# Keys and values of the first four pairs of a key-masked cross-attention made inside the recurrence sublayer before it

## The reference, cut to what matters

```python
x = x + rwkv(_layernorm(x), ...)                  # recurrence sublayer
x = x + xattn(_layernorm(x), ctx, ctx, mask, ...) # key-masked attention, 16 heads of 16

# xattn, per batch
q = (layernorm(x) @ Wq + bq) * 0.25
k = ctx @ Wk + bk          # depends on ctx and weights alone
v = ctx @ Wv + bv          # the same
p = softmax(q k^T + mask)  # per head
x = x + (p @ v) @ Wo + bo
```

## Time and profile before

| | us |
|---|---|
| median of 3 runs | 2873.56 (2870.24 to 2874.7) |
| the profiled execution's own time | 2876.9 |
| its span in the profile | 2875.1 |
| recurrence block, to the barrier behind it | some 245 |
| key-masked attention block, first steps' maxima to the last | 258.46 to 415.28 |
| busy over the span: TensorE, VectorE, ScalarE, GpSimd | 89%, 59%, 44%, 30% |

### The profile page before, as it was taken

The page is one execution under the profiler, slowest core; times in us unless marked ns, Lnnn a source line. Parts: engine busy times, 40 slices in busy tenths (PEclk is TensorE's granted clock), DMA queues, the critical chain, the costliest instruction groups (busy, mean ns, idle before and its releaser), DMA issues. The chain is left out here.

```text
span 2875.1 us, 49084 instructions
## 1 busy us (share of the span) xinstructions
PE 2545.3 (89%) x16401; PEld 1829.6 (64%) x16401; DVE 1705.5 (59%) x4509; ACT 1260.0 (44%) x3451; POOL 855.4 (30%) x687
## 2 busy tenths in 40 slices
PE   4998998989799889599998998978969899869997
PEld 2665665766544356477776776757956567449996
DVE  7875986588766644344445557873336578434443
ACT  2333654256455323444443445743432388324342
POOL 4533440045431044122221225641110044132222
PEclk8999999999899899799999999978989999989998
DMA  9001000000300333200001002042130210531110
GB/s 319 14 1 51 14 2 19 1 16 1 83 11 1 60 94 113 96 1 1 1 1 47 18 1 75 1 161 76 38 93 1 58 44 5 191 118 49 54 51 26
DMA packets 155268, 144.06 MB, mean 50 GB/s; under 512 B 62024, under 2 KB 139982, under 8 KB 154640
## 3 DMA queue, kind: packets, MB, share of 16 engines
q1 hardware_dynamic: 142880, 112.17, 13.6%
q0 software_dynamic: 10560, 27.19, 2.8%
q10 hardware_dynamic: 1584, 1.57, 0.2%
HBM read 99.70 MB, written 43.02 MB: 50 GB/s over the span
## 5 line engine op out<-in xcount | busy, mean ns | idle before, releaser
L979 POOL TENSOR_TENSOR room<-room 128x1024 f32<-128x1024 f32 x144 | 273.8, 1902 | 410.7 <-DVE room L912 410.6
L1454 PE MATMUL l3f_out<-room,Y 128*128 x624 | 141.0, 379 | 0.0
L906 DVE TENSOR_REDUCE room<-room 128x8 f32<-128x1024 f32 (+1 forms) x144 | 140.3, 975 | 0.8 <-ACT room L1057 0.8
L979 POOL TENSOR_TENSOR room<-room,Y 128x1024 f32<-128x1024 f32 x32 | 60.7, 1896 | 232.6 <-DVE Y L912 232.6
L3626 DVE SCALAR_TENSOR_TENSOR room<-l1x_v,room 128x512 f32<-128x512 f32 x128 | 86.9, 685 | 67.9 <-ACT room L3772 67.7
L1454 PEld LDWEIGHTS l3f_out<-room,Y 128*128 128x128 f32 x624 | 115.6, 190 | 14.2
L3772 ACT ACTIVATE room<-l1x_u 128x512 f32<-128x512 f32 x128 | 76.1, 598 | 77.2 <-PE l1x_v L3441 76.8
L1055 ACT ACTIVATE room<-l2a_scores,Y 128x128 f32<-128x128 f32 x256 | 71.0, 379 | 75.3 <-DVE Y L898 75.2
L1055 ACT ACTIVATE room<-l1a_scores,room 128x128 f32<-128x128 f32 x256 | 71.4, 386 | 58.3 <-DVE room L898 58.3
L1055 ACT ACTIVATE room<-l0x_scores,room 128x128 f32<-128x128 f32 x256 | 70.5, 384 | 59.2 <-DVE room L898 59.2
L623 PE MATMUL l2a_proj<-room 128*128 128x256 f32 x384 | 93.9, 387 | 0.0
(11 more groups left out here) (879 smaller groups left out, 6924.2 us busy)
## 6 DMA issues: line engine op xcount, KB each, us to landing
sorted_rows<-head SPq DMA_DIRECT2D x1, 16640.0 KB, 57.6
room<-in_L_ffn_w SPq DMA_DIRECT2D x16, 1024.0 KB, 12.6
room<-in_L_ffn_W SPq DMA_DIRECT2D x16, 1024.0 KB, 12.6
room<-in_ctx SPq DMA_DIRECT2D x32, 256.0 KB, 3.4
Y<-sorted_rows SPq DMA_DIRECT2D x62, 130.0 KB, 2.1
room<-sorted_rows SPq DMA_DIRECT2D x39, 130.0 KB, 2.1
room<-results SPq DMA_DIRECT2D x8, 512.0 KB, 7.1
room<-in_L_ffn_routed_w SPq DMA_DIRECT2D x4, 512.0 KB
```

The source lines that it names most:

```text
L906: dve.tensor_reduce(rsum[:, u % 2, 0:SUMMED], p[:, u % (TURN + 1), 0:SUMMED, :], AX.X, ALU.add)
L979: pool.tensor_tensor(p[:, u % (TURN + 1), :, :], p[:, u % (TURN + 1), :, :], rinv[:, u % (TURN + 1), :].unsqueeze(2).to_broadcast([P, HEAD ...
L1454: mm = pe.matmul(obank[n % 2][:, 0:D], hT[:, n % 2, f, :], chip.room[:, bass.ds(at + (SLOT // 2 + f * D), D)], start=(f == 0), stop=(f == ...
```

## The change

Three places change. In the recurrence block, the context rows of batches 0 to 7 (four pairs) and the attention's weights are loaded ahead of the zeroing transfer. TensorE transposes the rows (16 transposes), makes keys and values of the four pairs (eight products of eight instructions), and ScalarE copies them to new tiles `early_k` and `early_v` (8 copies of 128x512, and 4 of the transposed rows). Products 0 to 5 stand between `kvr(0, 1)` and `out(0, 0)`; products 6 and 7 stand on TensorE behind `out(0, 3)` and ahead of the transposes of group 1, and their copies stand on ScalarE behind the roots of the statistics and ahead of the squares of y. The rows and their transposes lie in `k2`, which is not in use yet.

In the attention block TensorE and ScalarE leave out c, k and v of pairs 0 to 3. VectorE's spreading of the keys (eight tensor_scalar) and its adding of the bias to the values (two tensor_tensor) stay, at the same places of the order, but read `early_k` and `early_v` in SBUF, and signal `spread`. SP loads no context rows for those pairs.

```diff
+    made = EARLY if t_ == "l0x" else 0                       # EARLY = 4
+    early_made = lambda x: x[0] < made and x[1][0] in "ckv"
...
         def wait_emptied(eng, x):
+            if early_made(x):
+                eng.wait_ge(spread, counted[x])
+                return
...
                 def load(g):
-                    if ctxsrc:
-                        if g >= 2:
+                    if ctxsrc and g >= made:
+                        if g >= made + 2:
...
                 def project(x):                              # TensorE
+                    if early_made(x):
+                        return
...
                 def empty(x):                                # VectorE
                     g, (kind, i) = x
-                    bank = wait_filled(dve, x)
-                    m = number[x]
+                    if early_made(x):
+                        bank, signal = (w.early_k if kind == "k" else w.early_v)[:, g, :], spread
+                    else:
+                        bank, m = wait_filled(dve, x), number[x]
+                        signal = emptied[m % 2]
...
                 def empty(x):                                # ScalarE
+                    if early_made(x):
+                        return
...
@@ rwkv_block
+        early_bank = [bank[i] for i in (5, 6, 7, 5, 6, 7, 7, 7)]
+        early_front = {3: 0, 4: 1, 5: 2, 6: 5, 7: 6}
...
             def _(sp):
                 w.load(sp, slice(3, None))
                 w.load_later(sp, chip.later_loaded)
+                prefetch.load(sp)
+                for g in range(EARLY):
+                    sp.dma_start(early_rows[:, g, :, :], chip.ins["ctx_1024"][g * PAIR:(g + 1) * PAIR].rearrange("b s d -> s b d")).then_inc(early_loaded, 16)
                 sp.dma_start(chip.sorted_rows.rearrange("(t p) d -> p t d", p=P), ...).then_inc(chip.rows_zeroed, 16)
-                if prefetch:
-                    prefetch.load(sp)
...
+                def turn_early(g):                           # TensorE
+                    pe.wait_ge(early_loaded, 16 * EARLY)
+                    if g < 2:
+                        pe.wait_ge(emptied[g], 1)
+                    else:
+                        pe.wait_ge(early_rowsT, g - 1)
...
+                def early_product(n):
+                    g, to = n // 2, early_bank[n]
+                    if n == 0:
+                        nw.wait(pe)
+                    if n in early_front:
+                        pe.wait_ge(early_kept, early_front[n] + 1)
+                    pe.wait_ge(early_rowsT, g + 1)
...
                 def out(a, j):
                     if n == 0:
                         pe.wait_ge(chip.later_loaded, 16 * len(w.later))
+                        pe.wait_ge(early_kept, 5)
...
                     if a < NG:
                         kvr(a, 1)
+                    if a == 0:
+                        turn_early(0)
+                        turn_early(1)
+                        for g in range(3):
+                            early_product(2 * g)
+                            early_product(2 * g + 1)
+                            if g + 2 < EARLY:
+                                turn_early(g + 2)
...
                         for j in range(GR):
                             out(a, j)
                     if a == 0:
+                        early_product(6)
+                        early_product(7)
+                        pe.wait_ge(early_rowsT, EARLY)
                         pe.wait_ge(hn1_ready, 2)
                         transposes(hn1, t1_fill(1))
...
                         exps(a, 1)                           # ScalarE
+                    if a == 0:
+                        keep_rowsT(0)
+                        keep_rowsT(1)
+                        for g in range(3):
+                            keep(2 * g)
+                            keep(2 * g + 1)
+                            if g + 2 < EARLY:
+                                keep_rowsT(g + 2)
...
                     act.preload_act_table(ACT.Sqrt)
                     if t == 0:
                         stats(slice(GR, NB), s[1])
+                        keep(6)
+                        keep(7)
```

More of the change, by code:

```diff
@@ L390 @@
 UNIT = 4
+EARLY = 4
 def attention_block(chip, plan, w, prefetch, have_stats, leave_twice):
@@ L451, in attention_block @@
             for x in here:
-                number[x] = len(number)
+                of = place if early_made(x) else number
+                of[x] = len(of)
+    counted = {x: sum(1 for y in place if y[1][0] != "c" and place[y] <= place[x]) for x in place}
     def by_scalar(f):
@@ L539, in attention_block @@
         ctx_loaded = [sem("ctx0_loaded"), sem("ctx1_loaded")]
+        spread = sem("spread")
         raw_loaded = [sem("raw0_loaded"), sem("raw1_loaded")]
@@ L614, in project @@
                     elif kind == "c":
[L615 removed]
+                        pe.wait_ge(ctx_loaded[g % 2], (g - made) // 2 * 16 + 16)
                         for kc in range(KC):
@@ L3880, in rwkv_block @@
         PER = 2 + FC // 2
+        nw = chip.next_weights
+        early_rows = k2[:, 0:EARLY, :].rearrange("p g (j d) -> p g j d", j=PAIR)
+        early_T = k2[:, EARLY:EARLY + 2, :].rearrange("p a (c t) -> p a c t", c=KC)
+        early_bank = [bank[i] for i in (5, 6, 7, 5, 6, 7, 7, 7)]
+        early_front = {3: 0, 4: 1, 5: 2, 6: 5, 7: 6}
+        early_loaded = sem("early_loaded")
+        early_turned, early_rowsT = sem("early_turned"), sem("early_rowsT")
+        early_filled, early_kept = sem("early_filled"), sem("early_kept")
         head = Head(chip, "rwkv", hn1) if chip.leave_head else None
@@ L3929, in kvr @@
                         mm.then_inc(kvr_filled, 1)
+                def turn_early(g):
[4 more added lines that the diff above has]
+                        pe.wait_ge(early_rowsT, g - 1)
+                    for kc in range(KC):
+                        for j in range(PAIR):
+                            mm = pe.transpose(bank[g % 2][:, (kc * PAIR + j) * P:(kc * PAIR + j + 1) * P], early_rows[:, g, j, kc * P:(kc + 1) * P], chip.ident[:, :])
+                    mm.then_inc(early_turned, 1)
+                def early_product(n):
[5 more added lines that the diff above has]
+                    pe.wait_ge(early_rowsT, g + 1)
+                    for i in range(2):
+                        for kc in range(KC):
+                            if n % 2 == 0:
+                                mm = pe.matmul(to[:, i * PT:(i + 1) * PT], nw.v["k"][:, kc, i * P:(i + 1) * P], early_T[:, g % 2, kc, :], start=(kc == 0), stop=(kc == KC - 1))
+                            else:
+                                mm = pe.matmul(to[:, i * D:(i + 1) * D], early_T[:, g % 2, kc, i * P:(i + 1) * P], nw.v["v"][:, kc, :], start=(kc == 0), stop=(kc == KC - 1))
+                    mm.then_inc(early_filled, 1)
                 def key2(c, f):
@@ L3951, in value2 @@
                     n = c * GR + j
+                    if n == 0:
+                        pe.wait_ge(early_kept, 2 * EARLY)
                     if j == 0:
@@ L4260, in exps, with keep_rowsT, keep @@
                     act.activation(rt[:, m, :], r_bank[:, :], ACT.Tanh, scale=0.5).then_inc(gate_ready, 1)
+                def keep_rowsT(g):
+                    act.wait_ge(early_turned, g + 1)
+                    if g >= 2:
+                        act.wait_ge(early_filled, 2 * (g - 2) + 2)
+                    act.copy(early_T[:, g % 2, :, :].rearrange("p c t -> p (c t)"), bank[g % 2][:, :]).then_inc(early_rowsT, 1)
+                def keep(n):
+                    act.wait_ge(early_filled, n + 1)
+                    act.copy((nw.early_v if n % 2 else nw.early_k)[:, n // 2, :], early_bank[n][:, :]).then_inc(early_kept, 1)
                 def relus(c, fs):
```

10 lines of the change are left out of this document (6 added, 4 removed).

## The result

| kernel | median, us | runs |
|---|---|---|
| before | 2874.13 (2870.24 to 2874.85) | 4 |
| after | 2889.08 (2887.12 to 2891.01) | 4 |

The ratio is 1.0047, interval 1.0035 to 1.0059: slower by over 0.2%. I forecast 2878.0 and a range up to 2884. The changed kernel was measured twice more, each time beside the kernel before: 1.0038 and 1.0039. So the change costs 11 to 15 us, and the forecast said 4.4. The profiled execution took 2887.1 us (span 2885.3) against 2876.9 (2875.1).

A forecast was written before the change was run, and what follows sets the result against it. TensorE was taken to set the attention's pace with VectorE 2 us behind a cycle, after which VectorE's order decides. Terms 2.4 - 5.2 + 7.2 = +4.4 us, added to the median, gave 2878.0 us; range 2864 to 2884.

The forecast's parts named there:

- step 3: Recurrence's first pass: uncovered products 6 and 7 hold up ScalarE's squares; VectorE's shift starts at 58.85, not 56.45, +2.4 us.
- step 4: Attention's opening: pair 0's c, k, v gone from TensorE, keys spread from SBUF, first scores earlier, -5.2 us.
- step 5: Attention steps making pairs 1 to 3: VectorE's spreads and adds from SBUF take turns with GpSimd, +7.2 us.
- second cycle: Four attention steps: k's spreads +1.5, v's adds +0.8, a wait for scores gone -0.2; +2.1 us.
- third cycle: Next four attention steps, same terms: k's spreads +1.5, v's adds +0.8, a wait gone -0.2; +2.1 us.
- the step behind: Attention, start of the cycle behind the third: TensorE is ahead there, -0.2 us.
- low clock: Slower rival: TensorE's clock falls in idle stretches ahead of `out` and the first scores; total +7.8 us, 2881.4; chance 0.22.
- r = 0: First step of an attention cycle: VectorE's wait of 0.17 us for scores goes, -0.2 us.
- Step 1: Loads ahead of the zeroing transfer: data in by about 27 us, zeroing some 10 us later, cost 0.
- Step 2: Early transposes and six products fit TensorE's idle 15.62 us ahead of `out`; cost 0, cover left 2 us.
- ports free: Faster rival in the attention: VectorE's spreads don't take turns with GpSimd; total -8.4 us, 2865.2; chance 0.18.
- half the turns: Faster rival in the attention: two v adds go back to back before GpSimd; total -0.5 us, 2873.1; chance 0.15.

The follow-up runs named there:

- fill_both: Changed kernel plus transposes nobody reads, at TensorE's idle places in the attention and 20 ahead of `out`; 2877.58 us, 1.0005 against the kernel before.
- order_only: Kernel before with only the attention's weights loaded ahead of the zeroing transfer; 2871.18 us, 1.0002 against the kernel before.
- early3_drip_q1_fill: Changed kernel: three early pairs, two spreads a step, q a step earlier, unread transposes in the attention's opening; 2878.49 us, 0.9976 against the kernel before.
- early3_drip: Changed kernel with three early pairs, two spreads in each step and v's adds, all right behind the maxima; 2869.88 us, 0.9983 against the kernel before.
- after_third: Changed kernel without any edit, run again as yardstick on the same chip; 2885.52 us, 1.0039 against the kernel before.
- after_again: Changed kernel without any edit, measured again in five rounds; 2884.09 us, 1.0038 against the kernel before.
- v_after_copy: Changed kernel with VectorE's v adds and k spreads behind its copy of the transposed probabilities, not ahead; 2877.51 us, 1.0018 against the kernel before.
- spread_first: Changed kernel with VectorE's k spreads and v adds right behind the maxima, ahead of the sums; 2877.30 us, 1.0011 against the kernel before.
- early3: Changed kernel with three pairs made early, without products 6 and 7 and their copies; 2878.40 us, 1.0014 against the kernel before.
- early3_drip_q1: Changed kernel with three early pairs, two spreads a step behind the maxima, and early pairs' q a step earlier; 2882.05 us, 0.9981 against the kernel before.
- after_fill: Changed kernel plus transposes nobody reads where TensorE idles in the attention's opening and first three pairs; 2891.37 us, 1.0016 against the kernel before.

## Why the prediction was wrong

The terms of my sum, beside what the trace of after and of fill_both (the same kernel with the clock held up at the filled places) has. Each is a difference to the kernel before, from the table above; the last two rows are measured starts, against 245.72 and 435.40.

| term | forecast | after | fill_both |
|---|---|---|---|
| step 3, the shift | +2.4 | +4.15 | +2.36 |
| step 4, first maxima | -5.2 | -4.00 | -4.91 |
| step 5, first cycle | +3.2 | +2.75 | +2.31 |
| second cycle | +2.1 | +2.93 | +1.52 |
| third cycle | +2.1 | +3.41 | +1.97 |
| the step behind | -0.2 | -0.14 | -0.14 |
| sum | +4.4 | +9.1 | +3.1 |
| start of the attention | | +2.95 | +2.88 |
| start of the block behind it | | +7.35 | +3.09 |

**With TensorE's clock up the sum was nearly right**: +3.1 by the trace and +3.45 by the medians of fill_both, against +4.4. **The step that failed** is the clock, in the attention. My rival "low clock" had the right mechanism and gave it 3.4 us and 0.22; it looked only at `out` and at the first scores. What it and the forecast both missed is in step 5, the line "r = 0: the wait of 0.17 goes, -0.2". Behind v's adds stands the copy L937, TensorE waits 2.1 us for it, and it no longer has v's product to fill that time. The steps r = 0 went from 4.12 and 4.98 to 5.44 and 6.46: +1.3 and +1.5 where I had -0.2 each. With the clock held up they are 3.98 and 4.84, -0.14 each. The places, each as after less fill_both: first scores 0.9, first step 1.4, the two steps r = 0 1.5 and 1.6, together 5.4 us. About 1 us of it is given back: in fill_both the third step of the first cycle takes 4.55 us and not 3.61, as TensorE idles 3.25 us ahead of it and the low level falls there instead. That leaves 4.3 us at the start of the next block (7.35 less 3.09).

**The sum of the shift and the rest is not the time.** The terms of after add up to 9.1 and its next block starts 7.35 later. Of the 4.15 us at the shift 2.95 are left at the attention, and 0.5 is gained behind the last maxima. Step 3 said of the shift's delay "nothing takes it back"; that was wrong for the part that the clock made. The eight kernels with products 6 and 7 start the attention at 248.5 to 250.5, those with `out` at 5.38 us no later (248.51, 248.56, 248.67, 250.52) than those with 3.7 (248.60, 248.69, 248.72, 248.88); the eight profiles without them start it at 244.2 to 247.5. The means are 2.9 us apart, so the delay by the two products did arrive, about as forecast.

**Step 1** held. The early transposes start at 30.93 (forecast 30.4), the zeroing transfer is issued at 23.12, 8.5 us later than before (I had 10), and order_only shows no price.

**Step 2** held: products done at 43.8 (44.3), the last copy at 44.5 (45.0), table load 1.28 us long and over at 45.8, ahead of the roots. But I called it "cost 0, cover left 2 us". The cover left is an idle stretch of TensorE, and `out` behind it ran at the low level at first, as it does in the kernel before.

**Step 3** was right in mechanism, and to 0.25 us in size where the clock stayed up: 58.81, 58.92, 58.94 and 59.09 in four kernels, forecast 58.85. With `out` at 5.38 us it is 60.4 to 60.7. The 6.14 us of my bound, which would have made it 4.8, did not come: the low level lasted for a part of `out` only. Without products 6 and 7 the length of `out` hardly matters. It took 3.69 us in early3_drip_q1_fill and 5.38 in early3_drip, and the shift started at 56.62 and 56.71, since the transposes of group 1 ahead of it start at 54.3 and 54.6.

**Step 4**: eight spreads in 2.67 us, forecast 2.7. They started 3.40 us behind the block's first matmul and not 2.92, and the scores 6.13 behind it, so 4.9 us and not 5.2 earlier. Then the low level took 0.9 us from the first scores and 1.4 from the next step.

**Step 5, the turns.** They were as I read them from the earlier trace rows; "ports free" (0.18) and "half the turns" (0.15) fell. The second spread waits out the residual's instruction, the second add waits out GpSimd's multiplication. The steps with k went up by 1.50, 1.17 and 1.17 us (forecast 1.9, 1.5, 1.5), those with v by 1.25, 0.54 and 0.84 (1.3, 0.8, 0.8). (The 5.2 us for the eight spreads were added up 0.1 short: 307.42, 0.25, 1.28 and seven times 0.33 end at 311.3. The group took 4.87 us in the third cycle.) The Trainium skill ("SBUF — State Buffer", section "SBUF: two separate sides") says that a VectorE instruction with two SBUF inputs or in a two-port mode and a GpSimd instruction hold the shared port pair for the whole instruction, whichever starts first. The trace agrees: a spread that takes 401 ns alone took 1653 and 1359 ns beside L994 and L976.

The spread's own price came out by the row and not by the Trainium skill's formula. One from SBUF took 401 ns (median 402 over 32), against 407 of L279, where the Trainium skill's cycle table ("VectorE: DVE Perf Modes", section on the TRN2 errata) gave an estimate of 194. Eight took 2.67 us against 3.71 from PSUM, a saving of 1.04 us.

**What stays open.** fill_both is 7.94 us under after_third by the medians, but the starts of the next block are only 3.4 us apart in these two profiles (4.3 against after). The rest isn't located. The profiles of the changed kernel differ among themselves at the same places (the third cycle's first step at 4.84 or 6.46 us), and a timed run can meet the low level where the profiled one did not; no run here counts that. In the profile of after 2.85 of its 10.2 us lie behind the attention, where nothing was changed; its two repeats had -3.1 and +4.5 us there, so this is scatter. Where the first measurement's 15 us, against 11 in the repeats, came from I can't tell.

## What to carry to other kernels

Work taken from TensorE uncovers the waits that the work had filled. Where TensorE then stands idle for 2 to 3 us, what follows may run at half the clock, and the next step pays it, on whichever engine waits for it. A delay is worth what is left of it at the end of the block, and filling one place can move the low level to the next. So for each stretch that a change empties, ask who waits behind it and what its matmuls cost at 1.2 GHz. Here useless transposes gave back 7.9 us of the 11.4 that the change cost. A VectorE instruction that is made to read SBUF instead of PSUM got cheaper by 0.13 us here (0.54 to 0.40) and took 1.3 to 2.0 us where it met one of GpSimd's, an add 2.12 and not 0.37. So place it where GpSimd is idle, and try a few in each step rather than eight in a row.

## What was not expected of the hardware

- The length of TensorE's idle stretch didn't settle its clock. Behind 2.88 us ahead of `out` the 16 matmuls took 5.38 us in after_again and 3.69 in v_after_copy, spread_first and after_third; behind 3.32 us they took 5.37 in early3 and 3.69 in early3_drip_q1. Behind 2.09 us four L657 took 1.92 us in one profile, behind 2.10 us 1.03 in another. I had read 2.59 us (low) and 2.15 us (high) in the earlier trace rows as two sides of a threshold; they are not.
- The low level came behind idle stretches of 2.1 us at times, and 6 to 20 transposes of 0.11 us each had TensorE at the high one for the work behind them at each place where they were put: the granted clock is 1.00 in the windows behind them. In the attention's opening they began at the low level themselves (16 took 2.92 us in fill_both, 1.91 in after_fill).
- The kernel before itself took 2872.75 to 2874.13 us on four occasions and 2884.74 on another chip. These 11 us are more than most of the effects here, so only runs beside the same kernel before can be compared.
